# A block kernel for attention and gated products: product order, block sizes and the last block

## The reference, cut to what matters

```python
X, Y = Z[:, :256], Z[:, 256:]                 # Z is layernorm(x)
scores = einsum('bdn,bdm->bnm', B_l @ X, C_l @ X)
att = relu(scores); att[:, -1, -1] = 0
X_out = X + A_l @ (X @ att)
Y_out = Y + r_l * (Y @ att)
x = x + layernorm(concat(X_out, Y_out))
g = layernorm(x) @ gate_w.T * gate_s          # 2048 -> 5632
u = layernorm(x) @ up_w.T * up_s
x = x + layernorm((silu(g) * u) @ down_w.T * down_s)
```

## Time and profile before

| what | us |
|---|---|
| median of 3 runs | 1046.83 (1046.16 to 1047.46) |
| the profiled execution | 1047.22 |
| its span on the slowest core, core 6 | 1045.7 |
| TensorE busy in it | 1007.7 (96%) |
| VectorE busy | 590.6 (56%) |
| ScalarE busy | 289.0 (28%) |
| GpSimd busy | 52.6 (5%) |

### The profile page before, as it was taken

The page is one execution under the profiler, slowest core; times in us unless marked ns, Lnnn a source line. Parts: engine busy times, 40 slices in busy tenths (PEclk is TensorE's granted clock), DMA queues, the critical chain, the costliest instruction groups (busy, mean ns, idle before and its releaser), DMA issues.

```text
span 1045.7 us, 12874 instructions; the slowest of 8 cores (1041.7 to 1045.7 us)
## 1 busy us (share of the span) xinstructions
PE 1007.7 (96%) x4797; PEld 465.4 (45%) x4893; DVE 590.6 (56%) x814; ACT 289.0 (28%) x427; POOL 52.6 (5%) x99
## 2 busy tenths in 40 slices
PE   6999999999999999999999999999999999999993
PEld 2445444444444444444444444444444444444441
DVE  4755666644654655555555555555554655554576
ACT  3645676622111111112112111111121111112266
POOL 0000000110001001001000010010010010001010
PEclk8999999999999999999999999999999999999997
DMA  8503331768326527428329229238248247339489
GB/s 234 113 1 121 121 122 81 139 110 134 61 41 105 97 41 118 84 41 133 69 41 154 48 46 156 41 61 141 41 71 131 43 82 118 57 65 166 116 126 196
DMA packets 18348, 101.09 MB, mean 97 GB/s; under 512 B 2160, under 2 KB 2288, under 8 KB 9456
## 3 DMA queue, kind: packets, MB, share of 16 engines
q0 software_dynamic: 13680, 75.77, 43.9%
q1 hardware_dynamic: 4608, 24.50, 6.9%
HBM read 152.95 MB, written 16.78 MB: 162 GB/s over the span
## 4 chain that ended last, share of the span: by engine, by line
PE 86%; DMA 4%; DVE 3%; ACT 3%; issue 2%; POOL 0%; DVEq 0%; ACTq 0%; POOLq 0%
PE ps L822 45%; PE ps L860 28%; PE ps L455 5%; DMA dwb<-dw 3%; PE ps L424 3%; PE ps L755 3%; DMA bcb<-bc 1%; DVE xr L520 1%; ACT lc L480 1%; PE ps L373 1%; DVE acc L849 1%; ACT lc L557 0%; ACT pc L345 0%; PE ps L404 0%; DMA xr<-xtop 0%
## 5 line engine op out<-in xcount | busy, mean ns | idle before, releaser
L822 PE MATMUL ps<-bop,wr 128*128 128x512 bf16 x2299 | 516.4, 379 | 2.8
L822 PEld LDWEIGHTS ps<-bop,wr 128*128 128x128 bf16 x2352 | 230.0, 98 | 277.4 <-issue 0.3
L860 PE MATMUL ps<-dwb,hdn 128*128 128x512 bf16 x1322 | 305.4, 379 | 2.2 <-DMA dwb<-dw 0.9
L875 DVE TENSOR_TENSOR acc<-acc,ps 128x2048 f32<-128x2048 f32 x70 | 160.2, 2288 | 213.6 <-PE ps L860 213.6
L860 PEld LDWEIGHTS ps<-dwb,hdn 128*128 128x128 bf16 x1344 | 131.2, 98 | 160.6 <-issue 3.2
L795 ACT COPY tmp<-ps 128x512 f32<-128x512 f32 x126 | 73.3, 582 | 347.9 <-PE ps L822 347.9
L803 DVE TENSOR_TENSOR tmp<-tmp,ps 128x512 f32<-128x512 f32 x126 | 86.5, 686 | 93.0 <-ACT tmp L795 46.5
L455 PE MATMUL ps<-att,xT 128*128 128x512 bf16 x497 | 116.4, 379 | 1.2 <-DVE xT L352 0.3
L782 DVE TENSOR_TENSOR wr<-wr 128x1024 bf16<-128x1024 bf16 x168 | 114.2, 686 | 4.7 <-DMA wr<-gu 0.2
L733 ACT ACTIVATE sg<-tmp,cpks 128x512 bf16<-128x512 f32 x63 | 45.5, 722 | 237.1 <-DVE tmp L803 237.1
L455 PEld LDWEIGHTS ps<-att,xT 128*128 128x128 bf16 x512 | 49.2, 98 | 57.3 <-issue 1.3
(11 more groups left out here) (96 smaller groups left out, 405.7 us busy)
## 6 DMA issues: line engine op xcount, KB each, us to landing
wr<-gu POOLq DMA_DIRECT2D x44, 1024.0 KB, 10.2
dwb<-dw POOLq DMA_DIRECT2D x42, 512.0 KB, 17.7
xr<-x SPq DMA_DIRECT2D x8, 1024.0 KB, 6.5
y<-xr SPq DMA_DIRECT2D x8, 1024.0 KB, 3.9
y<-acc POOLq DMA_DIRECT2D x6, 1024.0 KB, 9.0
xr<-xtop SPq DMA_DIRECT2D x4, 512.0 KB, 9.0
x1r<-y SPq DMA_DIRECT2D x2, 1024.0 KB, 7.0
dsB<-dsr SPq DMA_DIRECT2D x1, 1024.0 KB, 12.9
```

Source lines behind the costliest of these rows:

```text
L822: t = pg.pe(lambda e, c=c: e.matmul(ps[:, bk, :], wr[:, m % WS, ws, c * P:(c + 1) * P], bop[:, bs, c, :], start=(k in (1, 2, 5) and c == 0 ...
L860: t = pg.pe(lambda e, gi=gi, li=li, hc=hc: e.matmul(ps[:, banks[hc], :], hdn[:, gi % HS, tt * P:(tt + 1) * P], dw_at(gi)[:, hc * MQ:(hc + ...
L875: acc_t[tt] = pg.dv(lambda e: e.tensor_tensor(dst, dst, src, ALU.add), [t, acc_t[tt]])
```

## The change

It changes the numbers of idle matmuls, the place of some attention products relative to the transposes, the banks of the mixing transposes, the block sizes (6, seven of 4, and 10), the times and places of the loads of the down weight, and the order and pieces of the last norm. In the last norm the small steps go from VectorE to GpSimd and ScalarE, the last row tile's apart; row tiles 3 to 5 come in halves, and 4 to 7 get x from SBUF.

```diff
-BLKS = [4] * 9 + [8]
+BLKS = [6] + [4] * 7 + [10]
-        [("x1r", [P, 2, D], F32), ("junk", [P, D], BF16)])
+        [("x1r", [P, 4, D], F32), ("junk", [P, D], BF16)])
...
-    idle(17, [idle_t, xtop_ld[(0, 0)]])
+    idle(24, [idle_t, xtop_ld[(0, 0)]])
...
-    idle(8, [])
+    idle(4, [])
...
-                banks = (4 + 2 * g, 5 + 2 * g)
+                lo = 6 - 2 * g
+                banks = (lo, lo + 1)
...
     def dw_at(gi):
-        return {IT - 2: dwx0, IT - 1: dwx1}.get(gi, dwb[:, gi % DS, :])
+        if gi == IT - 1:
+            return dwy
+        return dwx[:, gi - (IT - 4), :] if gi >= IT - 4 else dwb[:, gi % DS, :]
...
+    for nt in range(8):
+        t0_mm(0, 3, nt)
     prep_tr(2)
...
-    t0(0, 3)
+    for nt in range(8, NT):
+        t0_mm(0, 3, nt)
+    epi(0, 3)
...
         if i + 1 < DT:
+            for nt in range(6):
+                t0_mm(i, 3, nt)
             prep_tr(i + 1, (0,))
-            for nt in range(4):
+            for nt in range(6, 10):
                 t0_mm(i, 3, nt)
             prep_tr(i + 1, (1,))
...
-        for nt in range(4 if i + 1 < DT else 0, NT):
+        for nt in range(10 if i + 1 < DT else 0, NT):
...
-        n_d = (0, 3, 3, 2)[n] if 0 < b and n < 4 else 0
-        done = (0, 0, 3, 6, 8)[min(n, 4)]
+        plan = (3, 3, 2, 0) if b == 1 else (0, 3, 3, 2)
+        n_d = plan[n] if 0 < b and n < 4 else 0
+        done = sum(plan[:n])
...
-        if b > 0 and n == 3:
+        if b > 0 and n == (2 if b == 1 else 3):
             for li in range(BLKS[b - 1]):
                 gi = BASE[b - 1] + li + DS
                 if gi < BASE[-1] + 2:
                     load_dw(gi, [hd_last[gi - DS]])
-        if m == NM - 4:
-            for gi in range(BASE[-1] + 2, IT - 2):
+        if m in (NM - 5, NM - 4):
+            for gi in range(2 * m - 42, 2 * m - 40):
                 load_dw(gi, [hd_last[gi - DS]])
         if m == NM - 3:
-            load_dw(IT - 2, [w_free[NM - 3]])
-            ds_ld = pg.dma("sync", "dsb", dsB[:, :], t_ds.ap(),
-                           [w_free[NM - 3]])
+            for gi in range(IT - 4, IT - 1):
+                load_dw(gi, [w_free[NM - 3]])
         if m == NM - 2:
             load_dw(IT - 1, [w_free[NM - 2]])
+            ds_ld = pg.dma("sync", "dsb", dsB[:, :], t_ds.ap(),
+                           [w_free[NM - 2]])
...
     def means(tt):
 
         c = slice(tt, tt + 1)
-        a = w_t[(tt, None)]
+        nm_t[tt] = pg.put("gpsimd", lambda e: e.tensor_scalar_mul(
+            nmW[:, c], wsum[:, c], -1.0 / D), [w_t[(tt, None)]], "GP")
+        a = pg.put("gpsimd", lambda e: e.tensor_tensor(
+            mqW[:, c], nmW[:, c], nmW[:, c], ALU.mult), [nm_t[tt]], "GP")
+        mq_t[tt] = pg.put("gpsimd", lambda e: e.tensor_scalar(
+            vw[:, c], mqW[:, c], -1.0, EPS, ALU.mult, ALU.add), [a], "GP")
...
+    two, four = ((0, 1), (2, 3)), ((0, 0), (1, 1), (2, 2), (3, 3))
+    PIECES = {3: two, 4: two, 5: two, 6: ((0, 1), (2, 2), (3, 3)), 7: four}
...
+        taken(tt, 0)
+        summed(tt, 0)
+        taken(tt, 1)
+        rstd(tt - 1)
+        if tt < LAST:
+            normed(tt - 1)
+            summed(tt, 1)
+            for j in range(2, len(PIECES[tt])):
+                taken(tt, j)
+                summed(tt, j)
+            joined(tt)
+            if tt - 1 not in x1_at:
+                add_up(tt - 1)
+            else:
+                store(tt - 1, 0, R)
+                store(tt - 1, R, D)
...
+    tt = LAST
     normed(tt - 1)
+    summed(tt, 1)
+    taken(tt, 2)
+    summed(tt, 2)
+    store(tt - 1, 0, R)
+    taken(tt, 3)
+    summed(tt, 3)
+    joined_last(tt)
     rstd(tt)
-    store(tt - 1, R, D, nrm_t[(tt - 1, None)], "y1")
-    bias(tt)
+    store(tt - 1, R, D)
     for k in range(4):
-        normed(tt, k)
-        store(tt, k * MQ, (k + 1) * MQ, nrm_t[(tt, k)], f"y{k}")
+        normed(tt, k * MQ, (k + 1) * MQ)
+        store(tt, k * MQ, (k + 1) * MQ)
```

More of the change, by code:

```diff
@@ L845, in build_nc, with acc_part @@
     part_t = {}
[L847 to L851, removed]
+    def acc_part(tt, ks, banks, name):
+        src = ps[:, banks[0]:banks[-1] + 1, :].rearrange("p a b -> p (a b)")
+        acc_t[(tt, name)] = pg.dv(lambda e: e.tensor_tensor(
+            acc[:, tt, ks], acc[:, tt, ks], src, ALU.add),
+            [part_t[banks[-1] % 4], acc_t[tt]])
+        for bk in banks:
+            tok_bank[bk] = (acc_t[(tt, name)],)
     def down_mm(b, tt, banks, order, sig):
@@ L980, in build_nc @@
     t = down_mm(b, 0, (0, 1, 2, 3),
-                [(li, hc) for li in range(6) for hc in range(4)], never)
+                [(li, hc) for li in range(8) for hc in range(4)], never)
     product(NM - 1, 4)
@@ L984, in build_nc @@
     t = down_mm(b, 0, (0, 1, 2, 3),
-                [(li, hc) for li in (6, 7) for hc in range(4)], never)
+                [(li, hc) for li in (8, 9) for hc in range(4)], never)
     acc_add(b, 0, (0, 1, 2, 3), t)
-    x1_at = {6: 0, 7: 1}
+    x1_at = {4: 0, 5: 1, 6: 2, 7: 3}
     x1_ld = {}
-    for tt in (6, 7):
-        x1_ld[tt] = pg.dma("sync", f"xo{tt}", x1r[:, x1_at[tt], :],
+    for tt, s in x1_at.items():
+        x1_ld[tt] = pg.dma("sync", f"xo{tt}", x1r[:, s, :],
                            t_y.ap()[tt * P:(tt + 1) * P, :],
@@ new lines, in joined, with joined_last @@
+    def joined(tt):
+        n = len(PIECES[tt])
+        t = None
+        for k in range(1, n):
+            in0 = wpart[:, tt, 0:1] if k == 1 else wsum[:, tt:tt + 1]
+            t = pg.put("gpsimd", lambda e, k=k, in0=in0: e.tensor_tensor(
+                wsum[:, tt:tt + 1], in0, wpart[:, tt, k:k + 1], ALU.add),
+                [w_t[(tt, n - 1)], t], "GP")
+        w_t[(tt, None)] = t
+        means(tt)
+    def joined_last(tt):
+        c = slice(tt, tt + 1)
+        a = pg.dv(lambda e: e.reduce_sum(
+            wsum[:, c], wpart[:, tt, :], AX.X), [w_t[(tt, 3)]])
+        b = pg.dv(lambda e: e.reduce_sum(
+            wsq[:, c], qpart[:, tt, :], AX.X), [sq_t[(tt, 2)], eps_q])
+        a2 = pg.dv(lambda e: e.scalar_tensor_tensor(
+            vw[:, c], wsum[:, c], -1.0 / (D * D), wsum[:, c],
+            ALU.mult, ALU.mult), [a])
+        mq_t[tt] = pg.dv(lambda e: e.scalar_tensor_tensor(
+            vw[:, c], wsq[:, c], 1.0 / D, vw[:, c], ALU.mult, ALU.add),
+            [a2, b])
@@ L1057, in store @@
[L1057 to L1069, removed]
-        means(tt)
@@ new lines, in cols, with taken, summed @@
+    def cols(tt, j):
+        lo, hi = PIECES[tt][j]
+        return slice(lo * MQ, (hi + 1) * MQ)
+    def taken(tt, j):
+        lo, hi = PIECES[tt][j]
+        acc_part(tt, cols(tt, j),
+                 [4 * (tt % 2) + k for k in range(lo, hi + 1)], j)
+    def summed(tt, j):
+        scaled(tt, cols(tt, j), wpart[:, tt, j:j + 1], j)
+        q = (qlast[:, :] if (tt, j) == (LAST, 3) else
+             qpart[:, tt, j:j + 1])
+        squares(tt, cols(tt, j), q, j)
+    eps_q = pg.dv(lambda e: e.memset(qpart[:, LAST, 3:4], EPS * D))
@@ L1077, in build_nc @@
     junk_t = [None]
-    for tt in range(DT - 2):
+    for tt in range(DT):
+        banks = (0, 1, 2, 3) if tt % 2 == 0 else (4, 5, 6, 7)
         if tt > 0:
[L1080 to L1091, removed]
-            normed(tt - 1)
-            add_up(tt - 1)
@@ L1096, in part @@
[L1096 to L1109, removed]
-    normed(tt - 1)
[L1111 to L1129, removed]
+            ends_at = [hi for lo, hi in PIECES.get(tt, ())]
+            t = down_mm(b, tt, banks, by_bank,
+                        lambda li, hc: hc in ends_at and li == BLKS[b] - 1)
+        if tt not in PIECES:
+            if tt > 0:
+                acc_add(b, tt, banks, t)
+                rstd(tt - 1)
+            whole(tt)
+            if tt > 0:
+                normed(tt - 1)
+                add_up(tt - 1)
+            continue
```

124 lines of the change are left out of this document (67 added, 57 removed).

## The result

The changed kernel takes 1056.35 us (median of 4 runs, 1056.04 to 1057.99) against 1047.06: a ratio of 1.0093, 95% interval 1.008 to 1.0105, so 9.7 us slower (8.4 to 11.0). I forecast 5.6 us slower, 1052.4, and a range to 1056, so the time lies outside it. The direction and the place of the largest loss are right, the size is too small. Some executions of either kernel run some per cent longer at a lower granted clock; every ratio here leaves them out.

The account below looks back on a forecast made before the run. TensorE, busy for 96% of the span, was taken as the bound, with gains only in waits and tail. Terms -0.6 + 1.5 + 5.2 + 0.4 - 0.2 - 0.7 = +5.6 us gave 1052.4 us, range 1044 to 1056.

Parts of the forecast that it names:

- Start: Ahead of the score products, more idle matmuls shorten TensorE's gap in front of gT: -0.6 us.
- the bound on the losing side: At the start, products begin as early as on core 3 but pay a half-rate stretch in full: 0.3 us worse.
- Attention: Products moved around the transposes and the mixing transposes' new banks make the loop later: +1.5 us, bounds -0.3 and +2.2.
- The closed ring: Attention loop's chain of waits over VectorE and ScalarE stays closed, so the four `pc` waits, 3.1 us, stay.
- Late weight tile: Weight tile 12 lands late behind six down tiles in GpSimd's queue, at 35.9 us from the first issue: +5.2 us.
- The slip of +2.1 behind the landing: After weight tile 12 lands, VectorE's two sums and `acc_add` hold the next `down` 2.1 us more.
- Clock: TensorE's standing still for the late weight tile brings a fall to half clock: +0.4 us.
- Tail: After the last matmul, the first quarter pass starts at +8.1 us instead of +8.8: -0.7 us.
- Refills and waits for `dwb`: Refills of four down tiles are six instead of eight, so waits on them shrink: -0.2 us.
- Rival 1: The weight tile lands in time, before 32.8 us, and the other terms sum to 0: 1046.8 us, chance 0.13.
- Rival 2: Waits for `pc` and the score go, passes do not hold the tail: 1037.6 us, or 1043 with late weight; chance 0.12.
- Rival 3: Last norm's five GpSimd steps come late; at 1.5 us each the last pass is 2.8 us later: 1055.2 us, chance 0.05.

Follow-up runs that it names:

- e2: Changed kernel with the attention part put back (products behind the transposes, mixing transposes in banks 4 to 7 rising): 1.0067 of the kernel before.
- e6: Changed kernel with refill split, passes first in the last block, mixing transposes' old banks, but the new order of products: 0.9987 of the kernel before.
- e1: Changed kernel with the refill at the end of step 8 cut to four down tiles, the other two issued behind weight tile 12: 1.0026 of the kernel before.
- e4: Changed kernel with 22 useless matmuls on TensorE ahead of product 1 of weight tile 12, where it stands still: 1.0089 of the kernel before.
- e3: Changed kernel with ScalarE's pass over the row tile before put ahead of the next one's squares in the last block: 1.0058 of the kernel before.
- e7: Changed kernel with refill split, attention part put back, passes first, and the second norm's small sums ahead of VectorE's xT eviction: 0.9948 of the kernel before.

## Why the prediction came out too small

- **Start, -0.6 forecast, -0.2 measured on the cores compared.** The gap in front of gT shrank as laid out, but core 2 paid 1.5 us at half clock in the score products. The case that I gave as the bound on the losing side (starts early, pays in full) was the commoner one: six of eight cores had a stretch at half clock in the score products.
- **Attention, +1.5 forecast, +1.6 measured; e2 shows 1.5.** The closed ring, the late bank and the last pass were all seen in the trace, and the bank that ScalarE frees late was the larger share. The sum came out better than its parts: for the case that no bank is late I had a gain of 0.3 us as the bound, and e6, where none is, shows a loss of 0.5.
- **Late weight tile, +5.2 forecast, 7.3 on the slowest core (5.3 of waiting and 2.0 in product 1): the step that failed.** The mechanism is shown by e1; the landing was mis-sized. I took 35.9 us, from 34.7 to 36.7; by core it came at 34.5 to 37.3, and the time of a kernel is that of its slowest core, so the late end counts. On that core a down tile added 3.4 us (25.2 less 18.4, for two), not the 3.1 that gave me 36.7, and the 0.8 that I took off for faster loads did not come. The need came at 32.3, not at 32.8. Together that is 1.9 of the 2.2 us by which the wait was longer (5.3 against 3.1). The slip of +2.1 behind the landing was right in size and wrong in form: the half clock took the place of the wait for `acc_add`.
- **Clock, +0.4 forecast.** Beyond the 2.0 just counted it is 0.3 us (388.20 to 391.95 for 16 matmuls instead of 3.45), and e4 shows no gain, clear of the noise, without the fall. The stretch of the weight products as a whole grew by 7.4 us, where these terms and the refills had made 5.4.
- **Tail, -0.7 forecast, +0.2 measured.** This term had the wrong sign. The events came in the order laid out, but later: `store(5)` began at -4.1 instead of -4.8, the first piece of row tile 7 at -1.8 instead of -2.5, the pass over row tile 6 ended at +4.5 instead of +3.4. ScalarE's small instructions, for which the prediction shows no price, stand in front of each pass: 0.3 us for each addition of a partial sum and 0.39 for the bias, 0.48 to the start of the pass. That they make the whole difference is an argument from the trace and not shown. That ScalarE's order, and not VectorE's load, sets the tail is shown by e3.
- **Refills and waits for `dwb`, -0.2 forecast.** They were 1.1 us instead of 0.9 on the cores compared, so this gained nothing.

In sum: 2.0 us from the stretch of the weight products, 0.9 from the tail, 0.4 from the start and 0.1 from attention, which is the way from 5.6 to the 9.0 us between the two profiled cores. The measured 9.7 has its own uncertainty of 1.3. Rival 1 (in time) is e1's kernel, not this one. Rival 2 (faster) needed the ring to break: it breaks by another edit, e7. Rival 3 shows only once the pass is earlier, in e3: there two of the five steps took 1.0 us each, less than the 1.1 up to which I had expected no cost, and it costs because ScalarE comes for the result earlier.

## What to carry to other kernels

Where loads share one queue in order, count for each refill what stands behind it and when that is needed; two loads of 512 KB issued one step later were worth 6 to 7 us, more than everything else in this change. The time is the slowest core's: take a landing's late end, not its middle. A chain that is closed over several engines is shortened by moving the instruction that closes it, not by moving work around the wait; look for one whose inputs have long been there but that stands behind a late one in its engine's list.

## What the runs showed of the hardware that was not expected

- A stretch at the 1.2 GHz level after a wait can be nearly free: product 1 took 3.7 us instead of 1.73 while VectorE worked off 3.7 us of its own (e4: no difference in time without the fall).
- GpSimd's additions of 128x1 take about 0.2 us alone, 0.35 us from start to start, and about 1.0 us beside VectorE's 128x1024 additions from SBUF.
- ScalarE's instructions on 128x1 differ: Exp 0.20 us (line 1058), Ln with a bias from SBUF 0.29 (1055), Identity with a bias from SBUF 0.28 to 0.30 (1050), Identity with scale and bias from SBUF 0.39 (1060). So here it is the number of operands from SBUF, and not the function, that goes with the time.
- With the same kernel the late cores change from run to run: over the four runs of the changed kernel the slowest core was 2, 0, 7 and 0, and core 7 had 1054.9 us in one and the shortest span of all, 1044.6, in another.
